# Scores, softmax and outputs of an edge group in one pass with a running maximum, gathers and scatters in turn

## What is computed

```python
h = jnp.maximum(_layernorm(x, axis=-1), 0.0)
x = x + _L0_gnn_ref(h, src, dst, edge_attr_3, edge_attr_10, edge_weight, W1, W2)   # ends in segment_sum over dst
h = jnp.maximum(_layernorm(x, axis=-1), 0.0)
# layer 1, h in place of x, 4 heads, inside _L1_gnn_ref:
s = jnp.einsum('hef,hef->eh', Q[:, receiver], K[:, sender]) * scale
m = jax.ops.segment_max(s, receiver, num_segments=n)
e = jnp.exp(s - m[receiver])
denom = jax.ops.segment_sum(e, receiver, num_segments=n)
num = jax.ops.segment_sum(e[..., None] * Vs, receiver, num_segments=n)
attn = num / denom                                  # 0 for nodes without edges
x = x + (h + attn.mean(axis=1) @ Wout)
```

## Time and profile before

| | |
|---|---|
| median of 3 runs (lowest, highest) | 1229.4 us (1228.82, 1230.21) |
| profiled execution: time, span | 1234.37 us, 1232.5 us |
| busy: PE, DVE, ACT, POOL | 711.3, 956.5, 631.8, 798.2 us |
| mean granted clock of PE | 0.718 |
| chain that ended last: DVE, PE, ACT, POOL | 39%, 23%, 9%, 7% |

### The profile page before, as it was taken

The page is one execution under the profiler, slowest core; times in us unless marked ns, Lnnn a source line. Parts: engine busy times, 40 slices in busy tenths (PEclk is TensorE's granted clock), DMA queues, the critical chain, the costliest instruction groups (busy, mean ns, idle before and its releaser), DMA issues.

```text
span 1232.5 us, 14731 instructions
## 1 busy us (share of the span) xinstructions
PE 711.3 (58%) x4352; PEld 530.8 (43%) x4352; DVE 956.5 (78%) x1703; ACT 631.8 (51%) x1661; POOL 798.2 (65%) x796
## 2 busy tenths in 40 slices
PE   1268787878787878787853465555452555552000
PEld 0157676767576767676742232322221222220000
DVE  6588989898989897888757888777898999997000
ACT  1457887787878787777645565655521011110000
POOL 6777777767766676660017777777730577776775
PEclk9867988889787878797875566776766555555555
DMA  5122121213111121110134242232100000000000
GB/s 119 37 54 61 28 58 29 57 31 91 39 46 41 43 64 50 42 23 23 46 124 173 82 113 69 84 99 72 41 21 12 7 10 11 10 11 10 11 10 8
DMA packets 40659, 60.38 MB, mean 49 GB/s; under 512 B 17361, under 2 KB 31077, under 8 KB 40324
## 3 DMA queue, kind: packets, MB, share of 16 engines
q1 hardware_dynamic: 12216, 46.86, 11.7%
q0 software_dynamic: 25184, 12.32, 6.4%
q10 hardware_dynamic: 3180, 0.26, 0.2%
HBM read 40.33 MB, written 19.37 MB: 48 GB/s over the span
## 4 chain that ended last, share of the span: by engine, by line
DVE 39%; PE 23%; DVEq 10%; ACT 9%; issue 8%; POOL 7%; SPq 2%; DMA 1%; POOLq 0%
PE sums L1065 12%; POOL out_dram L690 6%; DVE h1d_or_products L1404 6%; DVE run L1799 4%; ACT below L884 3%; ACT h1d_or_products L793 3%; PE tens L1055 3%; DVE run L1793 2%; DVE dstat L1423 2%; PE turnB L1041 2%; PE turnA L1041 2%; DVE halves_or_steps L1397 2%; DVE run L1804 1%; DVE features_or_scores L1702 1%; DVE features_or_scores L1707 1%
## 5 line engine op out<-in xcount | busy, mean ns | idle before, releaser
L690 POOL DMA_INDIRECT out_dram<-agg_or_stacks,scatter_index x196 | 195.1, 996 | 121.8 <-DVE agg_or_stacks L1809 61.0
L655 POOL DMA_INDIRECT x_rows<-in_x,src_index x196 | 201.0, 1025 | 93.0 <-issue 52.4
L681 POOL DMA_INDIRECT agg_or_stacks<-run_sums,sum_row_index x196 | 199.6, 1018 | 64.7 <-issue 54.9
L655 POOL DMA_INDIRECT x_rows<-in_x,dst_index x196 | 197.7, 1009 | 64.7 <-issue 64.4
L1404 DVE TENSOR_TENSOR h1d_or_products<-tens,hid 128x768 f32<-128x768 f32 x168 | 156.6, 949 | 15.6 <-PE tens L1059 15.0
L1065 PE MATMUL sums<-h1d_or_products,ident 128*128 128x192 f32 x896 | 151.7, 328 | 0.0
L1065 PEld LDWEIGHTS sums<-h1d_or_products,ident 128*128 128x128 f32 x896 | 145.0, 190 | 0.0
L1055 PE MATMUL tens<-w_scalar_stacks,agg_or_stacks 96*128 96x384 bf16 x196 | 59.4, 391 | 72.4 <-ACT h1d_or_products L793 42.7
L1207 PE MATMUL tens<-ubd,run 128*128 128x512 f32 x56 | 53.6, 1058 | 73.3 <-DVE run L1793 68.8
L1055 PE MATMUL tens<-w_scalar_stacks,stack_turned 96*128 96x384 bf16 x196 | 59.3, 391 | 51.5 <-ACT h1d_or_products L793 45.6
L793 ACT ACTIVATE h1d_or_products<-tens,hid 128x48 f32<-128x48 f32 x448 | 88.5, 356 | 0.1
(11 more groups left out here) (299 smaller groups left out, 2098.5 us busy)
## 6 DMA issues: line engine op xcount, KB each, us to landing
src_everywhere<-src_by_columns SPq DMA_DIRECT2D x14, 896.0 KB, 4.5
xin<-in_x SPq DMA_DIRECT2D x27, 449.5 KB
out_dram<-xin SPq DMA_DIRECT2D x27, 449.5 KB
x_rows<-in_x,src_index POOLq DMA_INDIRECT x196, 2.7
x_rows<-in_x,dst_index POOLq DMA_INDIRECT x196, 2.8
run<-run_sums SPq DMA_DIRECT2D x1, 3136.0 KB, 11.4
agg_or_stacks<-run_sums,sum_row_index POOLq DMA_INDIRECT x196, 3.4
out_dram<-agg_or_stacks,scatter_index POOLq DMA_INDIRECT x196, 2.1
```

The costliest lines, as they stand in the source:

```text
L655: nc.gpsimd.indirect_dma_start(xs[:, t, side, :], None, x, bass.IndirectOffsetOnAxis(ap=idx[:, t:t + 1], axis=0)).then_inc(s_gath[g % LEAD ...
L681: nc.gpsimd.indirect_dma_start(aggr[:, t, :], None, rs, bass.IndirectOffsetOnAxis(ap=ridx[:, t:t + 1], axis=0)).then_inc(s_rsg[g % LEAD2], 16)
L690: nc.gpsimd.indirect_dma_start(out, bass.IndirectOffsetOnAxis(ap=sidx[:, t:t + 1], axis=0), aggr[:, t, :], None, bounds_check=N - 1, oob_i ...
```

## The change

- The seven dense slices, the seven blocks of target rows and chunks 5 and 6 of the search (three parts each, THIRDS) are done in seven rounds ahead of the group loop; the target rows are scaled by their deviation there.
- `group2` now does scores, softmax and outputs of a group in one pass over 28 groups. A running maximum per partition and head is kept by a scan; numerators (4 heads x 32) and denominators are kept by one scan over 4 x 33 x 8 = 1056 columns, whose factor is exp(old maximum - new maximum) and 0 at the start of a segment. Group g's maximum and group g-1's weighting, scan and division stand interleaved in one iteration. The division gives each row's output at once; the scans and exchanges over all tiles are gone.
- PE turns target and source rows of a group together, and sums heads, target rows and residual (`sum_heads`) with the identity as one operand. ACT copies out the rows of each partition's first segment, for the crossing part, which is settled after the last group.
- Chunks 7 to 13 of the search lie in the first 14 groups; from chunk 5 on only the bank `sums` is used, so PE waits for ACT after every pair.
- POOL gathers LEAD2 = 12 groups, waits for the dense stores, and then scatters group g and gathers group g + 12 in turn.

Core of the diff (mostly added lines; what they replace is told above):

```diff
+    SLICE2 = range(len(SLICE1) + 2, len(SLICE1) + 2 + NBLK)
...
+    C2 = C1 + 2
...
+    LEAD2 = 12
+    NPS = NCHUNK - C2
...
+            load(GAP[1] + 2)
+            for j, d in enumerate(SLICE2):
+                store(d)
+                if d + 2 < ND:
+                    load(d + 2)
+                if j % 3 == 0 and C1 + j // 3 < C2:
+                    sp.wait_ge(s_S, C1 + j // 3 + 1)
+                    spread_src(C1 + j // 3 + 1)
+            for c in range(C2 + 1, NCHUNK):
+                sp.wait_ge(s_S, c)
+                spread_src(c)
...
+            def gather(g):
+                if past(g, LEAD2 - 1):
                     pool.wait_ge(s_bc, g - LEAD2 + 1)
-                nc.gpsimd.indirect_dma_start(
-                    aggr[:, t, :], None, rs, bass.IndirectOffsetOnAxis(ap=ridx[:, t:t + 1], axis=0)
-                ).then_inc(s_rsg[g % LEAD2], 16)
-
+                for t in range(g * GA, (g + 1) * GA):
+                    c, i = t // CT, t % CT
+                    if i == 0:
+                        pool.wait_ge(s_ridx, c + 1)
+                    elif i % 2 == 0 and c + 1 < C2:
+
+                        pool.wait_ge(s_cnt, (c + 1) * PAIRS + i // 2)
+                    nc.gpsimd.indirect_dma_start(
+                        aggr[:, t, :], None, rs, bass.IndirectOffsetOnAxis(ap=ridx[:, t:t + 1], axis=0)
+                    ).then_inc(s_rsg[g % LEAD2], 16)
+
+            def scatter(g):
+                pool.wait_ge(s_orow, g + 1)
+                for t in range(g * GA, (g + 1) * GA):
+                    nc.gpsimd.indirect_dma_start(
+                        out, bass.IndirectOffsetOnAxis(ap=sidx[:, t:t + 1], axis=0), aggr[:, t, :], None,
+                        bounds_check=N - 1, oob_is_err=False
+                    ).then_inc(s_osc, 16)
+
+            for g in range(LEAD2):
+                gather(g)
             pool.wait_ge(s_dout[0], 16 * (ND // 2))
             pool.wait_ge(s_dout[1], 16 * (ND // 2 + 1))
-            for t in range(T):
-                if t % GA == 0:
-                    pool.wait_ge(s_orow, t // GA + 1)
-                nc.gpsimd.indirect_dma_start(
-                    out, bass.IndirectOffsetOnAxis(ap=sidx[:, t:t + 1], axis=0), aggr[:, t, :], None,
-                    bounds_check=N - 1, oob_is_err=False
-                ).then_inc(s_osc, 16)
+            for g in range(NG):
+                scatter(g)
+                if fits(g + LEAD2):
+                    gather(g + LEAD2)
...
+            for j, d in enumerate(SLICE2):
+                dense_square(d)
+                dst_square(j)
+                dense_deviation(d)
+                dst_deviation(j)
+                if j < 3 * (C2 - C1):
+                    compare(C1 + j // 3, THIRDS[j % 3])
...
+            def exponentials(g, b):
+
+                act.wait_ge(s_sm, g + 1)
+                nc.scalar.activation(terms[:, b, :, FEAT, 1:], below_max, ACT.Exp)
+                nc.scalar.activation(decay[:, b, :, :, 1:], spread(max_step, 2, [P, HEADS, F1, GA]), ACT.Exp)
+                nc.scalar.copy(cols(max_all.rearrange("p h t -> p t h"), g),
+                               max_run[:, b, :, 1:].rearrange("p h t -> p t h")).then_inc(s_e, 1)
+
+            def first_segments(g, b):
+
+                act.wait_ge(s_num, g + 1)
+                for t in range(GA):
+                    last = nc.scalar.activation(
+                        head_rows[:, t, :], numer[:, b].rearrange("p h f t -> p (h f) t")[:, :, 1 + t], ACT.Copy,
+                        scale=last_of_first[:, g * GA + t:g * GA + t + 1])
+                last.then_inc(s_hb, 1)
...
+            def take_out(g):
+                act.wait_ge(s_osum, g + 1)
+                nc.scalar.copy(cols(aggr, g).rearrange("p t f -> p (t f)"), out_rows).then_inc(s_orow, 1)
+                if fits(g + 1):
+                    nc.scalar.copy(head_rows[:, GA, :], head_sum).then_inc(s_hkeep, 1)
+
+            def group2(g, b, pairs):
+
                 if fits(g + 1):
                     take_turned(g + 1, 1 - b)
+                    segment_steps(g + 1, 1 - b)
+                if past(g, 0):
+                    first_segments(g - 1, 1 - b)
+                exponentials(g, b)
+                if fits(g + 1):
+                    src_deviation(g + 1)
+                if fits(g + 2):
+                    src_square(g + 2, b)
+                if past(g, 0):
+                    take_out(g - 1)
+                if len(pairs) > 0:
+                    compare(C2 + g // 2, pairs)
...
+                    elif past(c, C1 - 1):
+                        pe.wait_ge(s_cnt, c * PAIRS + i)
...
+                    bank = found_in[i % 2] if c < C1 else sums
...
+            def sum_heads(g):
+
+                pe.wait_ge(s_hb, g + 1)
+                if past(g, 0):
+                    pe.wait_ge(s_orow, g)
+                    pe.wait_ge(s_hkeep, g)
+                for t in range(GA + 1):
+                    nc.tensor.matmul(head_sum, ident[:], head_rows[:, t, :], start=(t == 0), stop=(t == GA))
+                pe.wait_ge(s_val, g + 1)
+                for h in range(HEADS):
+                    nc.tensor.matmul(out_rows, ident[:], heads_out[:, h].rearrange("p t f -> p (t f)"),
+                                     start=(h == 0), stop=False)
+                nc.tensor.matmul(out_rows, ident[:], cols(h1d, g).rearrange("p t f -> p (t f)"), start=False, stop=False)
+                nc.tensor.matmul(out_rows.rearrange("p (t f) -> p t f", f=FEAT), ident[:], cols(xs, g)[:, :, 1, :],
+                                 start=False, stop=True).then_inc(s_osum, 1)
+
+            def group2(g, b, pairs):
                 if fits(g + 1):
                     turn_rows(g + 1)
+                    query(g + 1, 1 - b)
+                outputs(g, b)
+                if past(g, 0):
+                    sum_heads(g - 1)
+                if len(pairs) > 0:
+                    search(C2 + g // 2, pairs)
...
+            for j, d in enumerate(SLICE2):
+                if j == 3:
+                    decode(C1)
+                if j % 3 == 0 and C1 + j // 3 < C2:
+                    search_steps(C1 + j // 3)
+                dense_sums(d, dsum_p)
+                v.drain()
+                dense_centre(d, dsum_p)
+                dst_centre(j)
+                if past(j, 0):
+                    dst_scale(j - 1)
+                dense_variance(d)
+                dst_variance(j)
+                dense_scale(d, drec_p)
+                dense_add(d)
+            decode(C1 + 1)
+            dst_scale(NBLK - 1)
...
+            def weighted(g, b):
+                dve.wait_ge(s_y, g + 1)
+                v.tensor_tensor(terms[:, b, :, 0:FEAT, 1:],
+                                tens[1][:, 0:GA * P].rearrange("p (t h f) -> p h f t", t=GA, h=HEADS),
+                                spread(weights, 2, [P, HEADS, FEAT, GA]), ALU.mult).then_inc(s_yread, 1)
+            def accumulate(g, b):
+                if past(g, 1):
+                    dve.wait_ge(s_hb, g - 1)
+                v.tensor_tensor_scan(numer[:, b].rearrange("p h f t -> p (h f t)"),
+                                     decay[:, b].rearrange("p h f t -> p (h f t)"),
+                                     terms[:, b].rearrange("p h f t -> p (h f t)"), 0.0, ALU.mult, ALU.add
+                                     ).then_inc(s_num, 1)
+            def divide(g, b):
+                if past(g, 0):
+                    dve.wait_ge(s_osum, g)
+                v.tensor_tensor(heads_out, numer[:, b, :, 0:FEAT, 1:].rearrange("p h f t -> p h t f"),
+                                spread(den_rec, 3, [P, HEADS, GA, FEAT]), ALU.mult).then_inc(s_val, 1)
+            def group2(g, b, found):
+                if found and b == 0:
+                    search_steps(C2 + g // 2)
+                dve.wait_ge(s_q, g + 1)
+                v.tensor_tensor(hprod, tens[0][:, 0:GA * P].rearrange("p (t h f) -> p t h f", t=GA, h=HEADS),
+                                spread(cols(aggr, g), 2, [P, GA, HEADS, FEAT]), ALU.mult).then_inc(s_qfree, 1)
+                if past(g, 0):
+                    weigh(g - 1, 1 - b)
+                v.drain()
+                v.tensor_reduce(raw, hprod, AX, ALU.add)
+                if past(g, 0):
+                    weighted(g - 1, 1 - b)
+                dve.wait_ge(s_bd, g + 1)
+                v.reciprocal(cols(src_scale, g), cols(src_scale, g))
+                v.tensor_copy(score[:, :, 0:1], max_run[:, 1 - b, :, GA:])
+                v.drain()
+                if past(g, 0):
+                    accumulate(g - 1, 1 - b)
+                v.tensor_tensor(score[:, :, 1:], raw.rearrange("p t h -> p h t"),
+                                spread(cols(src_scale, g), 1, [P, HEADS, GA]), ALU.mult)
+                v.drain()
+                if past(g, 0):
+                    v.reciprocal(den_rec, numer[:, 1 - b, :, FEAT, 1:])
+                dve.wait_ge(s_far, g + 1)
```

(29 more changed lines are left out.)

527 lines of the change are left out of this document (185 added, 342 removed).

## The result

The changed kernel takes 1321.7 us (median of 4 runs, 1317.9 to 1327.2) against 1229.2; the ratio is 1.0736, with an interval of 1.0709 to 1.0763. The forecast was 1305, in a range of 1248 to 1348.

What follows compares the result with a forecast made beforehand. POOL was taken to bound the old kernel, the search half's engine chain to pace the new pass. 841 + 6.5 x 41.5 = 1111, + 187 = 1298, fix row 1.3, end 8.5: 1308, less 3.1: 1305 us; range 1248 to 1348.

Steps and rivals of the forecast that it cites:

- Preparation: Before the pass: seven rounds of about 12.3 us, every other one waiting 2 to 4; first row block out at 841.
- A group on DVE: VectorE's work for one group of the pass: 10.8 us, 12.2 in the first 14 groups with half a search chunk.
- thirteen steps of the search half: Pass from group 0 to 13: odd group 25.5 us, even 16, two groups 41.5; group 13 out at 1111.
- Behind group 13: POOL's remaining 15 groups to scatter and 3 to gather, with 26 us lost beside 14 scans: 187 us.
- From fix row to end: Kernel's tail: fix row 1.3 us, end 8.5; the median was then put 3.1 below the profiled span.
- rival B: Search half: PE stays at the low clock, 22.5 to 26 us a group, median 1327 to 1373; chance 0.17.
- C: Pass: POOL alone paces, decoding doesn't hold PE up, scans disturb little; median about 1250; chance 0.20.
- D: First output block: leaves at 817 if rounds never wait, POOL full from there; median 1216; chance 0.05 with its neighbourhood.
- E: Scatter and gather turns in the pass: DVE could run out of rows, 0 to 5 us; no separate chance given.
- F: ACT's table switches in the pass cost more than their load: 17 to 50 us longer, 1322 to 1355; chance 0.03.

Runs made afterwards that it cites:

- short rounds: Changed kernel with own early-loaded buffers for slices 23 to 25, and centring, variance and scaling of destination blocks 1 to 6 moved into the pass: 1293.2 us, 1.0481.
- the last run: Kernel combining all edits and an eighth early chunk (1236.2 us), plus early loads behind the carries, two banks in rounds, decoding mid-round, source rows before memsets: 1215.6 us, 0.9868.
- the 40 loads that went with the root: Changed kernel with ACT's square root of the source variances replaced by Relu, a function in every table: 1309.2 us, 1.0628.
- two banks: Changed kernel with the pass's search counts alternating between two PSUM banks and part counts of a half written ahead: 1298.7 us, 1.0560.
- late decoding: Changed kernel with decoding and the next step comparison moved to the end of the even group, behind its division: 1298.9 us, 1.0533.

## Why the prediction was right

The mechanism was right in each stage, and most terms within 3 us:

- Preparation: rounds were to end at 710, 724, 739, 757, 769, 786 and 798; they ended at 711, 725, 741, 758, 770, 788 and 801. First scatter 840.25 for 841. The short rounds show the waits for buffers and the blocks as its cause.
- A group on DVE: 10.8 forecast, 10.9 measured (scan 2.36 for 2.3, division 1.75 for 1.6). DVE's fix row was ready at 1281 for 1280, hidden as said.
- **The term that was off: thirteen steps of the search half.** The prediction took 6.5 x 41.5 = 269.8 us from group 0's row block to group 13's. But a long step (it holds the decoding) leads from each even group to the next odd one, so the thirteen are seven long and six short: by its own 25.5 and 16 they make 274.5. Measured were 279.8 us: long steps of 24.7 to 27.5, 25.9 on average, short ones of 16.1 to 16.7, 16.4 on average. So 4.7 of the 10 us are the count and 5.3 the size; since the first scatter was 0.8 early, group 13 was out at 1120 for 1111. ACT's copies of the blocks for groups 0 to 3 show two long steps and the short one between them:

```profile
838.97 0.34 ACT L983 COPY agg_or_stacks<-turnB 128x224 f32<-128x224 f32 x1 [1.39 <-PE turnB L1226]
863.70 0.32 ACT L983 COPY agg_or_stacks<-turnB 128x224 f32<-128x224 f32 x1
879.79 0.34 ACT L983 COPY agg_or_stacks<-turnB 128x224 f32<-128x224 f32 x1 [1.53 <-PE turnB L1226]
906.78 0.34 ACT L983 COPY agg_or_stacks<-turnB 128x224 f32<-128x224 f32 x1 [1.40 <-PE turnB L1226]
```

  In the long step of the chain above (27.0 us), decoding and comparison took 4.0 us behind the last pair, not 3.2, ACT's seven copies 3.1 behind the scan, not 2, and PE's sums ran at a mixed clock (granted 0.72 to 0.79 in the stages from 850 to 1100): 16 passes took 3.0 us there and 1.8 at 875.68.
- Behind group 13: 187.1 us for 187, and of it 25.8 lost to lengthened calls for 26. The forecast took 1.9 a scan from two single calls; the calls beside twelve of the last thirteen scans lose 1.9 to 2.0 each. That the sum agrees so well is in part luck: the 1.9 was made of 1.7 for the scan, averaged over the point at which it catches a call, and 0.2 for small instructions, and there were to be 14 scans; in truth the scan alone cost 1.9 to 2.0 (last section).
- From fix row to end 11.8 for 9.8, and the median stands 2.7 us above the profiled span where I took 3.1 below. 9, 2 and 6 are the 17 us between 1305 and 1321.7; why the end took 2 us more wasn't followed.

Of rival B the low clock was seen in part, but not the price: 21.5 us a group, not 22.5 to 26. C was right in that the decoding's place decides: moved, POOL paces. It was wrong on the scans: 52 us with POOL pacing, where it put 8. D's first condition failed by the 9 us between 831 and 840, and it wouldn't have been enough: with short rounds the first scatter left at 808 and the time was 1293, since POOL wasn't full and its calls were long. Only the last run, with both put right, came to D's 1216. E did not occur: DVE's groups stay at 10.5 to 11.3 us to the end. F: no idle time stands at a load (0.5 us before 28 of them), but the 40 loads that went with the root, 51.3 us, were worth 11 to 12 us, under a quarter of their length, so they lay partly on the path; the drain of 1.38 us per switch, which the Trainium skill, "ScalarE: Activation LUTs" (What ACT_TABLE_LOAD costs), adds to the load, isn't seen in the rows: the activation behind the load that ends at 1168.35 starts at 1168.37. On the port the runs agree with "SBUF — State Buffer" (SBUF: two separate sides), of the Trainium skill: the hold comes with the second SBUF operand, not with the length.

## What to carry to other kernels

When POOL issues a transfer for every 128 rows, a VectorE instruction with two SBUF operands holds the call that starts beside it until 0.8 us behind its own end: 1.9 to 2.0 us lost beside a scan of 2.36. Cut it where it can be cut (here 0.14 us more on VectorE gave back 1.3 on POOL per group), or keep one operand in PSUM, as the division does. In a pipeline of several engines the place of one short, waiting instruction in an engine's program can set the period: look for the engine that idles long before a wait that nothing urgent needs. Fusing two passes gains nothing by itself where the engine that issues the transfers has as many calls as before; what counts is when the first of the last kind can leave, and how many calls are done by then.

## What was not expected of the hardware

- The waits and the lengthened calls trade: as the waits in the pass fell from 28.9 to 3.4 (two banks) or 0 us (late decoding), the loss to long calls rose from 48.0 to 55.6 or 51.8 us. Part of a cost that hides under a wait returns when the wait goes.
- POOL's calls fell into step with the scans: seven scans from 1161.60 to 1227.22 us, some 11 us apart, each have a call of 2.91 to 2.99 us that starts 0.20 to 0.24 us behind them. The start isn't random, because the hold itself sets it: the held call ends 0.8 us behind the scan, the next starts 0.30 us later, six more follow at 1.29 us each (1165.09 to 1172.84), and the next scan has begun 0.23 us before the last of them. A random start, as I had taken it, would have cost less.
- Three loads of 450 KB beside the small transfers of the crossing sums put the first gather of sums off by some 6 us: POOL waited 4.3 to 4.4 us for the fix row's landing where it waited 1.4, and 3 to 4 us longer before it could send it.
